# Mixture-of-experts pair pipeline: GpSimd multiplies by the gate rows before VectorE, split products stay in PSUM, 20 pairs of 33 are split

## What is computed

```python
hg = jnp.einsum('ecd,efd->ecf', expert_in, w_gate)
hu = jnp.einsum('ecd,efd->ecf', expert_in, w_up)
expert_out = jnp.einsum('ecf,edf->ecd', jax.nn.silu(hg) * hu, w_down)
...
sparse = jax.ops.segment_sum(fg[:, None] * expert_out.reshape(-1, D), dst, num_segments=N + 1)[:N]
return shared_out + sparse.reshape(B, S, D)
```

## Time and profile before

| what | value |
|---|---|
| median of three runs | 717.83 us |
| span of the profiled execution | 716.0 us |
| TensorE matmul busy in it | 97% |
| VectorE, ScalarE, GpSimd busy | 73%, 49%, 65% |
| TensorE clock granted over the span | mean 0.995 of full speed |

### The profile page before, as it was taken

The page is one execution under the profiler, slowest core; times in us unless marked ns, Lnnn a source line. Parts: engine busy times, 40 slices in busy tenths (PEclk is TensorE's granted clock), DMA queues, the critical chain, the costliest instruction groups (busy, mean ns, idle before and its releaser), DMA issues.

```text
span 716.0 us, 9975 instructions
## 1 busy us (share of the span) xinstructions
PE 692.8 (97%) x3133; PEld 524.7 (73%) x3133; DVE 523.4 (73%) x1074; ACT 350.6 (49%) x609; POOL 466.5 (65%) x345
## 2 busy tenths in 40 slices
PE   7788899999999999999999999999999999999998
PEld 7666677777777777777777777777777777777775
DVE  5677686987768867887769877788678766674444
ACT  3543455446454374445553474544745435534432
POOL 5035477776677767685676776676775656676664
PEclk9999999999999999999999999999999999999999
DMA  5504232243323333333333433333333433334431
GB/s 204 226 1 128 71 118 104 85 133 105 111 106 114 114 108 99 120 113 102 118 103 101 128 103 103 118 110 109 114 105 102 125 103 105 115 112 124 138 123 60
DMA packets 48869, 80.17 MB, mean 112 GB/s; under 512 B 9520, under 2 KB 13744, under 8 KB 48816
## 3 DMA queue, kind: packets, MB, share of 16 engines
q1 hardware_dynamic: 47792, 77.44, 33.4%
q0 software_dynamic: 1024, 2.10, 1.2%
HBM read 76.35 MB, written 3.15 MB: 111 GB/s over the span
## 4 chain that ended last, share of the span: by engine, by line
PE 88%; DVE 4%; issue 3%; POOL 2%; ACT 1%; DVEq 0%; POOLq 0%
PE bank_y L467 16%; PE bank_g L481 8%; PE bank_g L482 8%; PE bank_g L483 8%; PE bank_u L483 8%; PE bank_u L481 8%; PE bank_u L482 8%; PE bank_y L464 4%; PE bank_y L462 4%; PE bank_y L461 4%; POOL hid L1040 1%; PE bank_f L408 1%; PE bank_f L386 1%; PE bank_f L402 1%; PE bank_f L445 1%
## 5 line engine op out<-in xcount | busy, mean ns | idle before, releaser
L1040 POOL TENSOR_TENSOR hid<-hid,gate_rows 128x512 f32<-128x512 f32 x256 | 374.2, 1470 | 195.4 <-DVE hid L881 193.0
L623 ACT ACTIVATE hid<-bank_g 128x512 f32<-128x512 f32 x264 | 156.6, 599 | 264.4 <-PE bank_g L483 261.8
L881 DVE TENSOR_TENSOR hid<-hid,bank_u 128x512 f32<-128x512 f32 x264 | 178.7, 681 | 128.3 <-PE bank_u L483 78.2
L481 PE MATMUL bank_g<-x_hi,gate_hi 128*128 128x512 f32 x264 | 142.9, 541 | 0.0
L467 PE MATMUL bank_y<-hid,w_down 128*128 128x512 f32 x272 | 138.7, 591 | 0.0
L887 DVE TENSOR_TENSOR hid_lo<-hid,hid_hi 128x512 fp32r<-128x512 f32 x128 | 110.2, 861 | 2.4 <-ACT hid_hi L629 2.4
L482 PE MATMUL bank_g<-x_hi,gate_lo 128*128 128x512 f32 x264 | 104.5, 396 | 0.0
L483 PE MATMUL bank_g<-x_lo,gate_hi 128*128 128x512 f32 x264 | 104.5, 396 | 0.0
L481 PE MATMUL bank_u<-x_hi,up_hi 128*128 128x512 f32 x264 | 103.9, 393 | 0.1
L483 PE MATMUL bank_u<-x_lo,up_hi 128*128 128x512 f32 x264 | 103.8, 393 | 0.0
L482 PE MATMUL bank_u<-x_hi,up_lo 128*128 128x512 f32 x264 | 103.8, 393 | 0.0
(11 more groups left out here) (209 smaller groups left out, 857.1 us busy)
## 6 DMA issues: line engine op xcount, KB each, us to landing
gate_rows<-gates_dram SPq DMA_DIRECT2D x512, 128.0 KB, 2.9
w_down<-down_t_dram SPq DMA_DIRECT2D x3, 704.0 KB, 14.5
out_dram<-later SPq DMA_DIRECT2D x7, 256.0 KB, 3.1
hid<-gate_t_dram SPq DMA_DIRECT2D x2, 704.0 KB, 5.8
gates_dram<-gates_t SPq DMA_DIRECT2D x8, 128.0 KB, 2.2
gate_rows<-up_t_dram SPq DMA_DIRECT2D x1, 704.0 KB, 5.7
later<-up_t_dram SPq DMA_DIRECT2D x1, 704.0 KB, 9.9
raw<-gate_t_dram SPq DMA_DIRECT2D x1, 704.0 KB, 11.0
```

The costliest lines, as they stand in the source:

```text
L481: pe.matmul(o, w_hi[name][:, p, :], x3_hi[par][:, :], start=True, stop=False)
L623: act.activation(hid[:, slot(par, p), :], bank_g[(p + par) % 2][:, :], ACT.Silu).then_inc(sem("silu"), 1)
L881: dve.tensor_tensor(hid[:, s, :], hid[:, s, :], bank_u[(p + par) % 2][:, :], ALU.mult)\
L1040: pool.tensor_tensor(hid[:, s, :], hid[:, s, :], gate_rows[:, row, :], ALU.mult)\
```

## The change

The 16 odd split pairs become 20 listed ones: `PLAIN_PAIRS` are 0, 1, 2, 3, 4, 8, 12, 16, 18, 24, 26, 28 and 30, all others are split. For a plain pair the order of work stays. For a split pair:

- GpSimd multiplies silu's `hid` by the gate rows as soon as silu is done; it doesn't wait for VectorE.
- VectorE's new `dve_product` multiplies that by the up bank and writes the result back into the up bank. It waits for GpSimd (`gated`) and stands at the head of step p+1, in front of the late and early pieces of that step.
- ScalarE's `act_hi` waits for the product, reads the up bank and stands at the end of step p+1; it stood two steps behind.
- VectorE's `dve_lo` reads the up bank and `hid_hi` and stands at the head of step p+2, in front of the next pair's product.

The up bank of a split pair is thus held until its low part is made. There are three up banks for this, used by pairs in turn, and one `bank_y`: the first `down` of a batch waits until ScalarE has copied the previous batch's sum out, which moves from step 5 to step 4. `hid_hi` and `hid_lo` get three slots each. `down_hi` and `down_lo`, the split down weights, are made in nine instructions each instead of one, since the split pairs no longer lie at an even distance. Some SBUF is saved by aliases (`vals`, `decay_full`) and by a broadcast column of ones.

```diff
+PLAIN_PAIRS = (0, 1, 2, 3, 4, 8, 12, 16, 18, 24, 26, 28, 30)
+SPLIT_PAIRS = tuple(p for p in range(PAIRS) if p not in PLAIN_PAIRS)
...
-        bank_u = [bank(f"bank_u{i}") for i in range(2)]
-        bank_y = [bank(f"bank_y{i}") for i in range(2)]
+        bank_u = [bank(f"bank_u{i}") for i in range(3)]
+        bank_y = bank("bank_y")
...
+            if p == 0:
+                wait(pe, "ffn_t", b)
...
+            for name, o in (("gate", bank_g[q % 2][:, :]), ("up", bank_u[q % 3][:, :])):
+                if name == "gate":
+                    wait(pe, "silu", q - 1)
+                else:
+                    b3, p3 = pairs_back(b, p, 3)
+                    if b3 is not None and is_split(p3):
+                        pe.wait_ge(sem("hid_lo"), split_count(b3, p3))
+                    elif b3 is not None:
+                        pe.wait_ge(sem("up_used"), plain_count(b3, p3))
...
+        def act_hi(act, b, p):
+
+            act.wait_ge(sem("product"), split_count(b, p))
+            wait(act, "down_done", split_slot_freed(b, p))
+            act.activation(hid_hi[:, split_slot(b, p), :], bank_u[(PAIRS * b + p) % 3][:, :], ACT.Copy)\
                .then_inc(sem("hid_hi"), 1)
...
-                    act.activation(down_hi[:, :, :], odd_pairs(w_down), ACT.Copy).then_inc(sem("down_hi"), 1)
+                    for j, pairs in split_runs():
+                        last = act.activation(down_hi[:, j, :], w_down[:, pairs, :], ACT.Copy)
+                    last.then_inc(sem("down_hi"), 1)
...
+        def dve_product(dve, b, p):
+
+            q = PAIRS * b + p
+            dve.wait_ge(sem("gated"), q + 1)
+            dve.wait_ge(sem("pe_up"), q + 1)
+            u = bank_u[q % 3][:, :]
+            dve.tensor_tensor(u, hid[:, slot(b % 2, p), :], u, ALU.mult).then_inc(sem("product"), 1)
+
+        def dve_lo(dve, b, p):
+            k = split_slot(b, p)
             dve.wait_ge(sem("hid_hi"), split_count(b, p))
...
+        def dve_split(dve, b, p):
+
+            b2, p2 = pairs_back(b, p, 2)
+            if b2 is not None and is_split(p2):
+                dve_lo(dve, b2, p2)
+            b1, p1 = pairs_back(b, p, 1)
+            if b1 is not None and is_split(p1):
+                dve_product(dve, b1, p1)
...
             for p in range(PAIRS):
+                dve_split(dve, b, p)
                 if p == DVE_AT["result"] and not first:
...
-                if p >= AHEAD - 1 or not first:
+                if (p >= AHEAD - 1 or not first) and not is_split(p):
                     dve_up(dve, b, par, p)
...
-                pool.wait_ge(sem("up_used"), q + 1)
+                if is_split(p):
+                    pool.wait_ge(sem("silu"), q + 1)
+                else:
+                    pool.wait_ge(sem("up_used"), plain_count(b, p))
```

More of the change, by code:

```diff
@@ L281, in split_lo @@
                 dve.wait_ge(sem("down_hi"), 1)
-                dve.tensor_tensor(down_lo[:, :, :], odd_pairs(w_down), down_hi[:, :, :].bitcast(F32), ALU.subtract)\
-                   .then_inc(sem("down_lo"), 1)
+                for j, p in split_runs():
+                    last = dve.tensor_tensor(down_lo[:, j, :], w_down[:, p, :], down_hi[:, j, :].bitcast(F32),
+                                             ALU.subtract)
+                last.then_inc(sem("down_lo"), 1)
         def gate_row_loads(sp, b, r):
@@ L463, in down @@
                 pe.wait_ge(sem("hid_lo"), split_count(b, p))
-                pe.matmul(y, down_hi[:, j, :], hid_lo[:, k, :], start=False, stop=False).then_inc(sem("down_done"), 1)
+                pe.matmul(y, down_hi[:, j, :], hid_lo[:, k, :], start=False, stop=(p == PAIRS - 1)).then_inc(sem("down_done"), 1)
             else:
@@ L475, in gate_up @@
                     pe.wait_ge(sem(f"split_lo{CHUNK_OF[n, p]}"), 1)
[L476 to L480, removed]
+            if b == 0 and p == 2:
+                pe.wait_ge(sem("h"), 2)
+            for name, o in (("gate", bank_g[q % 2][:, :]), ("up", bank_u[q % 3][:, :])):
[7 more added lines that the diff above has]
+                        pe.wait_ge(sem("up_used"), plain_count(b3, p3))
                 pe.matmul(o, w_hi[name][:, p, :], x3_hi[par][:, :], start=True, stop=False)
@@ L541, in _ @@
             for p in range(PAIRS):
[L542 removed]
+                pe_early(pe, 0, p, first_banks)
                 if p == PE_AT["exp_t"]:
@@ L622, in act_silu @@
             wait(act, "down_done", q - RING + 1)
[L623 to L629, removed]
+            act.activation(hid[:, slot(par, p), :], bank_g[q % 2][:, :], ACT.Silu).then_inc(sem("silu"), 1)
+        def act_hi(act, b, p):
+            act.wait_ge(sem("product"), split_count(b, p))
+            wait(act, "down_done", split_slot_freed(b, p))
+            act.activation(hid_hi[:, split_slot(b, p), :], bank_u[(PAIRS * b + p) % 3][:, :], ACT.Copy)\
                .then_inc(sem("hid_hi"), 1)
@@ L647, in act_sequence @@
                 act_silu(act, b, par, p)
[L648 to L651, removed]
+                b1, p1 = pairs_back(b, p, 1)
+                if b1 is not None and is_split(p1):
+                    act_hi(act, b1, p1)
         def split_hi(act, at):
@@ L681, in _ @@
             last = BATCHES - 1
-            for p in range(PAIRS - SPLIT_LAG, PAIRS):
-                if is_split(p):
-                    act_hi(act, last, 1, p)
+            if is_split(PAIRS - 1):
+                act_hi(act, last, PAIRS - 1)
             act.wait_ge(sem("down_done"), PAIRS * BATCHES)
@@ L982, in _ @@
             last = BATCHES - 1
-            for p in range(PAIRS - SPLIT_LAG, PAIRS):
-                if is_split(p):
-                    dve_lo(dve, last, 1, p)
+            dve_split(dve, last, PAIRS)
+            if is_split(PAIRS - 1):
+                dve_lo(dve, last, PAIRS - 1)
             dve.wait_ge(sem("stored"), 16 * BATCHES)
```

80 lines of the change are left out of this document (47 added, 33 removed).

## The result

| | before | after |
|---|---|---|
| median | 718.0 us (716.8 to 719.8, 4 runs) | 750.1 us (749.1 to 751.7, 4 runs) |
| ratio after/before, 95% interval | | 1.0448 (1.0424 to 1.0471) |
| span of the profiled execution | 716.0 us | 747.5 us |

The change costs 4.5%: the side that was forecast, but 14 us more than the 736 forecast. In the profiled spans it is +31.5 where the sum said +18.5.

The account below looks back on a forecast made before the run. TensorE, 88% of the chain, was taken as the bound. Seven sequences at +2.7 (18.9), −0.7 for the eighth and +0.3 gave +18.5 on 716.0: 734.5, median 1.8 above, 736; own range 725 to 746, full range 711.5 to 758.

Parts of the forecast that it names:

- the loop of plain and split pairs: Steps 24 to 30: plain product, two GpSimd multiplies, split product, late piece, next plain product wait in turn; chance 0.60.
- The loops: Pairs 24 to 26 take 5.00 us against TensorE's 4.34; pairs 26 to 28 take 5.34 against 4.32.
- The late start: VectorE starts the router group around step 24 late: 0.9 us taken, at least 0.4, far end 1.8.
- delays of steps 12 to 20: Delays from ScalarE's copies queuing behind `xn`'s copy, not made up by step 24; part of the 0.9 us start delay.
- at the gates: VectorE's two gate operations, held up by GpSimd's multiplies, end 2.4 us late per sequence; 1.83 without the hold-up.
- at step 6: TensorE's existing 0.49 us gap for the decayed state's inputs partly absorbs VectorE's lateness: 0.25 per sequence (0 to 0.49).
- at the splits: Each added split saves TensorE 0.17 us in `down`; four more per batch save 0.68, of which 0.34 counted per late-piece sequence.
- Beginning and end: Preparation adds 0.9 to 1.8 us, sequence 0 saves 1.5 at best; net +0.3, from −1.5 to +1.8.
- eighth sequence: It has no late pieces; its loop of 3.95 us is below TensorE's two pairs, so the saving of 0.7 stays.
- The faster case: Rival: the loop doesn't bind and TensorE keeps its stream, 717.8 − 5.4 = 712 us; chance 0.20.
- a lower clock: Rival: new waits lower TensorE's clock, one such stretch per sequence adding 12 us: 748; chance 0.14 shared with dear PSUM.
- a dear product in PSUM: VectorE's product costs 1.30 us in PSUM instead of 0.60, adding 15: 751; chance 0.14 shared with the clock.

Follow-up runs that it names:

- the old order with the same 20 pairs: The changed kernel's 20 splits, three up banks and single accumulator, but VectorE's product first into SBUF, then GpSimd, as before the change: 717.1 us.
- the sum moved: The changed kernel with GpSimd's sum hx at step 14 instead of step 12: 743.1 us, ratio 1.0353.
- 23 to 30 plain: The changed kernel with pairs 23 to 30 all plain (16 splits) and GpSimd's sum hx at step 14: 718.9 us, ratio 1.0018.
- product behind in 3 steps: The changed kernel with GpSimd's sum hx at step 14 and VectorE's product behind the late pieces in steps 24, 26 and 28 alone: 732.1 us.
- first experiment: The changed kernel with VectorE's product of every split pair behind the late and early pieces of its step: 749.4 us, ratio 1.0431.
- 18 splits: The order of before the change, with three up banks, one accumulator and the change's list with 20 and 22 plain too: 713.45 us, ratio 0.9943.

## Why the prediction came out as it did

**Bound and mechanism: right.** TensorE did bind, nothing had slack for a new wait, and the loop of plain and split pairs is the cause (25, 27, 29 plain removes its waits; the old order with the same 20 pairs leaves 0.30 and 0.56, in steps 25 and 30). That VectorE "never waited for GpSimd" before holds for the products only: `xn` (L746), for one, waited for GpSimd's `inv`, 2.3 us in all.

**The loops: right within 0.3 us.** Measured by the starts of the plain products: 395.54 − 390.61 = 4.93 where 5.00 was worked out, 400.65 − 395.54 = 5.11 where 5.34 was. In the second, the piece `chosen` took 1.21, from 0.60 behind product 27 to plain product 28 (399.44 to 400.65), where 1.39 was taken.

**The late start: right in size, in part by luck.** The router group started 1.03 after TensorE's router matmul, and 2.10 after it now: +1.07, where 0.9 was taken. The 0.9 was multiply 23 (0.4) and delays of steps 12 to 20 carried on. Those are not carried on: with the sum moved, step 12 falls to 2.82 and step 25 stays at 2.96. What stands in their place on the timeline is the wait for a slot of `hid_hi`, which the sum nowhere has. Where product 23 isn't in front of the group (23 to 30 plain; product behind in 3 steps), the group still starts 1.49 and 1.50 after the router matmul, 0.46 late by low part 22 alone; product 23 adds the other 0.6. No run has more slots. The late start reaches TensorE partly by a way that the sum didn't name: silu 24 is later too, and the gate bank waits 0.59 for it. Against the router matmul, the up matmuls of 26, 28 and 30 came 1.25, 1.84 and 2.60 late (worked out: 1.05, 1.71, 2.73), the gates' transposition 3.50 (3.3).

**The step that failed: which late pieces the new wait reaches.** The sum followed the wait at the head of the step only through steps 24 to 31, where the pieces crowd. The same wait stands in front of `xn` in step 11, which TensorE reads in step 12, and it is the same sight as at step 24: an exponential holds silu up on ScalarE, and the multiply is added behind it. "The delays of steps 12 to 20" are named there, but only as a delay carried on to step 24; that TensorE itself waits for a piece at step 12 was not priced. Measured +1.17 in each of six sequences and +0.36 in the seventh, which carries fewer pieces: 7.4 (the first sequence counted like the others), the largest part of the 13 that were missing. The hold-up of a VectorE operation by GpSimd was weighed for product and low part, where it doesn't act, and for the gates, but not for the pieces beside them, where it does: the run with the sum moved took back 1.0 of the 1.17.

**The rest of the 13, by size.** Per sequence, 0.2 at the gates, 0.09 at step 6 (−0.16 instead of −0.25), 0.05 at the splits (0.15 to 0.16 each instead of 0.17), and 0.2 in hundredths over the other steps: 0.5, over seven sequences 3.7. First sequence 0.45 more than the others. Beginning and end +1.4 instead of +0.3; eighth sequence −0.44 instead of −0.7. With 7.4 this makes 13.

**The bounds.** The product into PSUM was taken at the cheap end, rightly:

```profile
L933 DVE TENSOR_TENSOR bank_u<-hid,bank_u x160: 677/686/697, 74.6 to 740.6; 128x512 f32<-128x512 f32 x160
L938 DVE TENSOR_TENSOR hid_lo<-bank_u,hid_hi x160: 675/690/694, 78.6 to 742.0; 128x512 fp32r<-128x512 f32 x160
L1100 POOL TENSOR_TENSOR hid<-hid,gate_rows x256: 1267/1293/2770, 65.4 to 739.3; 128x512 f32<-128x512 f32 x128
```

The single lines after, as the earlier trace rows: the product into PSUM takes 0.686, the low part never more than 0.694 (2.179 before), the multiply 1.293 at the median (1.370 before). One multiply took 2.770, at 73.0 in the first sequence; the next longest took 1.490. The Trainium skill (SBUF — State Buffer, section "Who interferes with whom") lets a VectorE instruction with at most one SBUF input run beside GpSimd when it is outside the 2-port performance modes, a condition that the prediction left out. The products and low parts agree: 209 of the 320 overlapped an operation of GpSimd, and none took more than 0.697. The operations of `xn` and L846, which read no second tile, were held up beside GpSimd (2.30 and 1.24); no run here shows whether they fell under that condition.

**The rivals.** The faster case fell: the loop binds. The lower clock did not come: 1.00 in the middle stretch, and 0.83 at 60 to 80 us as before, though TensorE waits some 0.6 us several times per sequence. The range (711.5 to 758) held 750, but by its width: what stood near 750 in it were a lower clock (748) and a dear product in PSUM (751), and neither came. The forecast's own range (725 to 746) did not hold it, because its high end contained no term for a piece that the list of causes left out.

## What to carry to other kernels

Before an operation of a slow engine is put in front of an operation of a fast one, walk the loop that arises through every in-order queue (here product, multiply, multiply, product, late piece) and set its length against the pitch of the bound engine; busy shares of 94, 72, 50 and 56% showed nothing of it. Then list *every* operation queued behind the new wait, in every step and on every engine, with the time at which its reader wants it: the waits that this prediction and its first experiment missed (`xn` for step 12, ScalarE's copy for step 13) were two such readers. Buffers belong to the walk: the three slots of `hid_hi` made ScalarE wait for TensorE just ahead of the router group. And a saving on the bound engine is worth choosing by place: 18 splits gained 0.6% where 20 gained nothing.

## What was not expected of the hardware

- An operation on 128x4 elements (L846, its input and output in SBUF; 0.17 at the shortest in the same run) took 1.24 us at 397.59, until GpSimd's block of multiplies (396.30 to 398.81) was over. Here its size didn't count, but what GpSimd was in the midst of.
- The four operations of `xn` took 1.27 where GpSimd was through after 0.6 us, 1.93 beside one multiply in the kernel before, and 2.30 where GpSimd's sum followed at once on its multiply.
- The clock in the preparation differs between profiled executions: in the first 20 us the table of stretches grants 1.00 before, 0.91 after, 0.83 in the old order with 20 or 18 pairs. At 40 to 60 us it grants 1.00 in the old order with 20 pairs and 0.74 with 18 (rows below), and the first step began at 51.0 and 53.1 (before: 48.3), though the preparation of the two differs by two pairs' weights at most. With 18 pairs this goes together with the profiled span (714.1), which shows less gain than the sequences do, and a difference of 2 us between profiled spans says little. Why it comes and goes stays open.

The first two lines are of 20 pairs, the last two of 18:

```profile
0.00:20.00 20.00, 15.82 (x90) 14.59 (x91) 9.22 (x44) 6.93 (x9) 10.68 (x18) 0.83 0.63 220
...
40.00:60.00 20.00, 15.74 (x106) 13.22 (x107) 16.51 (x65) 7.08 (x11) 6.21 (x6) 1.00 0.03 9
...
0.00:20.00 20.00, 15.99 (x87) 14.79 (x88) 9.63 (x45) 6.93 (x9) 10.67 (x18) 0.83 0.62 220
...
40.00:60.00 20.00, 18.32 (x96) 15.08 (x97) 15.11 (x65) 7.07 (x11) 5.44 (x5) 0.74 0.03 7
```
